# A cross-attention and feed-forward block: bias rows added by VectorE, or by accumulating SBUF transfers that GpSimd issues

## The reference

```python
x = x + (softmax(clip(q k^T * scale)) v) @ Wo + bo        # q from layernorm(x), k and v from the context; 16 heads
h   = layernorm(x) @ W1 + b1                              # 512 -> 2048
q   = h + (cos(theta)*w_re + sin(theta)*w_im) * (w_im * sin(theta + 0.1*h)) * 0.1
out = x + relu(q) @ W2 + b2                               # 2048 -> 512
```

## Time and profile before

| | |
|---|---|
| three runs | 1977.26, 1973.52, 1974.97 us; median 1974.97 us |
| span of the profiled execution | 1974.9 us (the page gives no other time for it; the span runs from the first to the last instruction) |
| TensorE | busy 1953.4 us, 99% of the span; mean granted clock 0.998 |
| VectorE | busy 1542.5 us, 78% |
| ScalarE | busy 1262.7 us, 64% |
| GpSimd | busy 517.0 us, 26%, nearly all of it in the first third |
| DMA | 441.29 MB, mean 223 GB/s; SP's queue takes 71.3% of the 16 engines' span |
| `add_row_bias` on DVE (L1827) | 28 instructions, 33.5 us |
| `add_last_bias` on DVE (L1835) | 32 instructions, 38.9 us |

### The profile page before, as it was taken

The page is one execution under the profiler, slowest core; times in us unless marked ns, Lnnn a source line. Parts: engine busy times, 40 slices in busy tenths (PEclk is TensorE's granted clock), DMA queues, the critical chain, the costliest instruction groups (busy, mean ns, idle before and its releaser), DMA issues.

```text
span 1974.9 us, 27897 instructions
## 1 busy us (share of the span) xinstructions
PE 1953.4 (99%) x9162; PEld 1620.3 (82%) x9162; DVE 1542.5 (78%) x2360; ACT 1262.7 (64%) x2132; POOL 517.0 (26%) x365
## 2 busy tenths in 40 slices
PE   9999999999999999999999999999999999999999
PEld 7788888888887788777888888788788888878887
DVE  8988888888876986888588768868858876886773
ACT  6767767767754876667367557647746755764762
POOL 6877777777774321000000000000000000000000
PEclk9999999999999999999999999999999999999999
DMA  7455565565545999778778878877977887786745
GB/s 239 147 164 158 160 165 146 163 173 150 156 111 161 333 351 298 255 224 256 277 236 246 263 257 249 256 268 236 260 282 233 244 261 258 241 262 221 236 150 192
DMA packets 347459, 441.29 MB, mean 223 GB/s; under 512 B 165552, under 2 KB 201392, under 8 KB 347312
## 3 DMA queue, kind: packets, MB, share of 16 engines
q1 hardware_dynamic: 346448, 439.44, 71.3%
q10 hardware_dynamic: 864, 0.04, 0.0%
HBM read 347.90 MB, written 91.23 MB: 222 GB/s over the span
## 4 chain that ended last, share of the span: by engine, by line
PE 76%; DVE 11%; ACT 6%; issue 4%; POOL 2%; DMA 1%; SPq 0%; DVEq 0%; ACTq 0%; POOLq 0%
PE psum L1985 25%; PE psum L1987 24%; PE psum L1986 24%; PE psum L2078 3%; DVE frac L1789 1%; ACT turns L1363 1%; DVE stats L1472 1%; ACT x_sb L1163 1%; ACT frac L1339 1%; DVE act_lo L1810 1%; DVE temps L1515 1%; DVE hid L1803 1%; DVE x_sb L1827 1%; ACT act_hi L1391 1%; DVE late_hid L1784 1%
## 5 line engine op out<-in xcount | busy, mean ns | idle before, releaser
L1985 PE MATMUL psum<-w_ring,act_hi 128*128 128x512 f32 x1024 | 400.3, 391 | 2.0 <-DVE act_lo L1810 1.4
L1987 PE MATMUL psum<-w_ring,act_lo 128*128 128x512 f32 x1024 | 398.6, 389 | 0.0
L1986 PE MATMUL psum<-w_ring,act_hi 128*128 128x512 f32 x1024 | 398.4, 389 | 0.0
L1985 PE MATMUL psum<-xo,w_ring 128*128 128x512 f32 x784 | 308.4, 393 | 5.5 <-ACT p_sb L1346 4.5
L1986 PE MATMUL psum<-xo,w_ring 128*128 128x512 f32 x784 | 305.9, 390 | 0.0
L1987 PE MATMUL psum<-xo,w_ring 128*128 128x512 f32 x784 | 305.9, 390 | 0.0
L886 POOL TENSOR_TENSOR rstd<-var_eps,minus_half 128x4 f32<-128x4 f32 x32 | 38.6, 1207 | 948.9 <-DVE var_eps L1479 944.1
L1985 PEld LDWEIGHTS psum<-w_ring,act_hi 128*128 128x128 f32 x1024 | 192.2, 188 | 49.2 <-issue 10.1
L1789 DVE SCALAR_TENSOR_TENSOR frac<-frac,turns 128x512 f32<-128x512 f32 x256 | 173.7, 690 | 74.5 <-ACT frac L1339 74.5
L1376 ACT ACTIVATE frac<-frac 128x512 f32<-128x512 f32 x256 | 156.6, 627 | 109.6 <-DVE frac L1789 109.6
L1987 PEld LDWEIGHTS psum<-w_ring,act_lo 128*128 128x128 f32 x1024 | 192.2, 188 | 40.3
(11 more groups left out here) (188 smaller groups left out, 4291.4 us busy)
## 6 DMA issues: line engine op xcount, KB each, us to landing
w_ring<-w2s SPq DMA_DIRECT2D x240, 512.0 KB, 3.7
w_ring<-w1s SPq DMA_DIRECT2D x392, 256.0 KB, 3.6
x_sb<-turn_dram SPq DMA_DIRECT2D x58, 512.0 KB, 6.2
res<-in_x SPq DMA_DIRECT2D x64, 256.0 KB, 3.7
x_dram<-res SPq DMA_DIRECT2D x64, 256.0 KB, 3.0
acc<-x_dram SPq DMA_DIRECT2D x16, 1024.0 KB, 7.1
x_sb<-in_x SPq DMA_DIRECT2D x15, 1024.0 KB, 6.1
x_sb<-x_dram SPq DMA_DIRECT2D x15, 1024.0 KB, 7.4
```

What stands on the lines that cost most here:

```text
L1985: pe.matmul(o, a_hi, b_hi, start=first, stop=False, skip_group_check=resumed)
L1986: pe.matmul(o, a_hi, b_lo, start=False, stop=False, skip_group_check=resumed)
L1987: return pe.matmul(o, a_lo, b_hi, start=False, stop=last, skip_group_check=resumed)
```

## The change

For the pairs' tiles, 26 transfers issued by POOL take the place of 52 DVE additions. Each is an SBUF-to-SBUF transfer with `accum_op=ALU.add`: its source is `bo_row` or `b2_row`, repeated for the four blocks, and its destination a whole tile of 1 MB (`x_sb[0]`, `x_sb[1]`, `acc[0]` or `acc[1]`) that already holds the loaded rows. Twelve go to `x_sb` (tiles 4 to 15) and fourteen to `acc` (tiles 2 to 15). DVE's consumers wait for the new semaphores `rows_added` and `out_added`. Tiles 0 to 3 of the row bias and tiles 0 and 1 of the output bias stay on DVE and POOL as before. Four pairs of semaphores are merged into one each, with the counts adjusted, which changes no instruction's place.

```diff
-            for T in range(4, TILES):
-                rsqrt(TILES + T)
+            def add_row_bias_by_dma(T):
+                pool.wait_ge(x_in[T % 2], x_loads(TILES + T))
+                pool.dma_start(x_sb[T % 2][:], bo_row[:].unsqueeze(1).to_broadcast([P, NB, C]), accum_op=ALU.add)\
+                    .then_inc(rows_added[T % 2], 16)
+
+            def add_last_bias_by_dma(T):
+                pool.wait_ge(acc_in[T % 2], 16 * (T // 2 + 1))
+                pool.dma_start(acc[:, T % 2], b2_row[:].unsqueeze(1).to_broadcast([P, NB, C]), accum_op=ALU.add)\
+                    .then_inc(out_added[T % 2], 16)
+
+            for T in range(1, FFN_PAIRS):
+                more = T + 1 < FFN_PAIRS
+                if more:
+                    add_row_bias_by_dma(2 * T + 2)
+                add_last_bias_by_dma(2 * T)
+                if more:
+                    add_row_bias_by_dma(2 * T + 3)
+                    rsqrt(TILES + 2 * T + 2)
+                    rsqrt(TILES + 2 * T + 3)
+                add_last_bias_by_dma(2 * T + 1)
...
+                    elif T > TILES + PLAIN + 1:
+                        dve.wait_ge(rows_added[T % 2], 16 * ((T - TILES) // 2 - 1))
                     elif T > TILES:
                         dve.wait_ge(x1_whole, whole_rows(T - TILES, n // 2))
...
-                    dve.wait_ge(acc_biased, 2 * T + n // 2 + 1)
+                    if T >= PLAIN:
+                        dve.wait_ge(out_added[T % 2], 16 * (T // 2))
+                    else:
+                        dve.wait_ge(acc_biased, 2 * T + n // 2 + 1)
...
-                    if p == (0 if T > 1 else 2):
-                        for half in range(2):
-                            add_last_bias(2 * T, half)
...
-                    if more and p == 0:
-                        for half in range(2):
-                            add_row_bias(2 * T + 2, half)
-                    if more and p in (2, 3):
-                        add_row_bias(2 * T + 3, p - 2)
-                    if p in (5, 7):
-                        add_last_bias(2 * T + 1, p // 6)
```

More of the change, by code:

```diff
@@ L298, in xattn_ffn @@
         vbd_in = sems("vbd_in", PAIRS)
-        bq_scaled = sem("bq_scaled")
+        bq_scaled = par_sin = sem("bq_scaled")
         mean_step, mean_moved = sem("mean_step"), sem("mean_moved")
-        par_step, par_sin = sem("par_step"), sem("par_sin")
+        par_step = sem("par_step")
         x_in = sems("x_in", XBUFS)
@@ L312, in xattn_ffn @@
         q_full_done, halves_done = sem("q_full_done"), sem("halves_done")
-        xn0_done = sem("xn0_done")
         x1_whole = sem("x1_whole")
@@ L322, in xattn_ffn @@
         y_psum, y_done = sem("y_psum"), sem("y_done")
-        nan_step, nan_psum, nan_count = (sem(n) for n in ("nan_step", "nan_psum", "nan_count"))
-        guard_done, last_done = sem("guard_done"), sem("last_done")
+        nan_step, nan_psum = sem("nan_step"), sem("nan_psum")
+        xn0_done = nan_count = nan_step
+        guard_done = last_done = sem("guard_done")
         fix_in, fix_add, fix_out = sem("fix_in"), sem("fix_add"), sem("fix_out")
@@ L336, in xattn_ffn @@
         acc_in, acc_biased, b2_biased = sems("acc_in", 2), sem("acc_biased"), sem("b2_biased")
+        rows_added, out_added = sems("rows_added", 2), sems("out_added", 2)
         SPLIT0 = 2 * KC
@@ L761, in load_rows @@
                 if T >= GUARDED:
-                    sp.wait_ge(last_done, 1)
+                    sp.wait_ge(last_done, 2)
                     for blk in range(NB):
@@ L978, in _ @@
                             .then_inc(w_lo_done, 1)
-            pool.wait_ge(nan_count, 1)
+            pool.wait_ge(nan_count, 4)
             count = pool.alloc_register("rows_without_nan")
@@ L1413, in _ @@
                         act.wait_ge(x1_stored[blk], 16 * TILES)
-                    act.wait_ge(last_done, 1)
+                    act.wait_ge(last_done, 2)
                 for n in later_chunks(j):
@@ L1685, in _ @@
                         dve.tensor_tensor(not_nan[:], squares[:], squares[:], ALU.is_equal).then_inc(nan_step, 1)
-                        dve.wait_ge(nan_step, 1)
+                        dve.wait_ge(nan_step, 2)
                         dve.tensor_reduce(row_ok[:], not_nan[:], AX_X, ALU.min).then_inc(nan_step, 1)
@@ L1848, in operand_sum @@
                 dve.tensor_tensor(PLACE[name], PLACE[a], PLACE[b], ALU.subtract).then_inc(t_done, 1)
-            dve.wait_ge(par_sin, 1)
+            dve.wait_ge(par_sin, 2)
             dve.wait_ge(par_step, PAR_REDUCED + 4)
@@ L1902, in _ @@
                         dve.wait_ge(x1_stored[blk], 16 * TILES)
-                    dve.wait_ge(last_done, 1)
+                    dve.wait_ge(last_done, 2)
                 for n in later_chunks(j):
@@ L2151, in _ @@
                 if i == GROUPS:
-                    pe.wait_ge(nan_step, 2)
+                    pe.wait_ge(nan_step, 3)
                     pe.matmul(psum[0:1, 0, 0:1], row_ok[:], ones[:], start=True, stop=True).then_inc(nan_psum, 1)
@@ L2215, in second @@
                 m.then_inc(f_psum, 1)
-            pe.wait_ge(nan_count, 1)
+            pe.wait_ge(nan_count, 4)
             pe.wait_ge(xn_done, TILES + 1)
```

## The result

The changed kernel took 1961.62 us (median of 4 runs, 1960.05 to 1962.60), the kernel before 1974.56 us beside it (4 runs, 1973.52 to 1977.26): a ratio of 0.9931 with a 95% interval of 0.9919 to 0.9943. That is faster by some 13 us (11 to 16 by the interval), where 9.8 had been predicted.

What follows compares the result with a forecast made beforehand. TensorE was taken to set the end, losing 14.2 us to VectorE's full list; 7.6 us back in pairs 2 to 6 and 2.2 in pair 1, with transfers at 0, took 1974.9 to 1965.1 us, range 1960 to 1997.

Steps and rivals of the forecast that it cites:

- full return: Rival: all 14.2 us that TensorE loses from 867 us on come back, giving 1960.7 us; chance 0.1.
- C: Start of step 6 of a pair: TensorE loses some 0.3 us, of which half, 0.15, was to return.
- D: Start of a pair's sweep: TensorE loses some 0.7 us waiting for late `act_lo`, of which 0.5 was to return.
- Pair 1: The first pair, from 867 us on: TensorE loses 3.2 us, of which 2.2 was to return.
- VectorE's busy time: Whole kernel: 52 bias additions of about 1.2 us go, so VectorE's busy time falls by some 62 us.
- A: Start of step 2 of a pair: TensorE loses 0.38 us with the matmul behind it; all was to return.
- B: Start of step 5 of a pair: TensorE loses 0.49 us waiting for ScalarE's `p_sb`; all was to return.
- GpSimd: Issues 26 transfers, otherwise idle in the pairs; even 3 us each ends by step 1, delaying nothing wanted earlier.
- The new waits: Consumers of accumulated tiles: 1 MB taken to land in 15 us, between 7 and 40; only 40 would delay statistics.
- The DMA cost of 0: Near a pair's start: SP's queue keeps up at half of 394 GB/s, 7.6 us to spare for weight slots, costing 0.
- The starved ring: Rival: late weight slots stall TensorE 3.9 us in step 1 or 2, plus 1.3 slow clock; 1996 us, chance 0.30.
- Relief that isn't used: Rival: ScalarE is late by itself, so little returns; 1971.6 us or later; chance 0.14, shared with a small starvation.

Runs made afterwards that it cites:

- odd_rows: Kernel before, with only the row bias of each pair's odd tile added by transfer (VectorE's additions of steps 2 and 3 gone): 1963.33 us, ratio 0.9944.
- even_outs: Kernel before, with only the output bias of each pair's even tile added by transfer (two of VectorE's step 0 additions gone): 1966.46 us, ratio 0.9957.
- odd_outs: Kernel before, with only the output bias of each pair's odd tile added by transfer (additions of steps 5 and 7 gone): 1967.97 us, ratio 0.9960.
- outs_x2: Changed kernel with each even tile's output-bias transfer issued twice, 1 MB more per pair: 1977.87 us, ratio 1.0012.
- moved: Kernel before, no bias transfers, with the even tile's two output additions in steps 4 and 6 instead of step 0: 1979.71 us, ratio 1.0024.
- outs_only: Changed kernel with only the fourteen output-bias transfers kept; VectorE adds the row bias again: 1960.10 us, ratio 0.9922.
- spaced: Changed kernel with the even tile's output-bias transfer issued behind the pair's first `rsqrt`, so only two accumulations meet the loads: 1962.05 us, ratio 0.9936.
- spaced_tile1: Changed kernel with the even output-bias transfer behind the pair's first `rsqrt`, and tile 1's output bias also added by transfer: 1962.00 us, ratio 0.9934.

## Why the prediction was right, and what was mis-sized

The mechanism is the predicted one: TensorE at the pace of one matmul per 0.2267 us is the floor, the losses are VectorE's lag, and they go. The sum was 9.8 us; the traces show 14.2 back, the new stall of 0.6 already taken off, and the medians 13. That is "full return", which had 0.1 of the chances. So the mechanism was right, and the term that was mis-sized is the share of each loss that comes back (C, D and pair 1 below).

- **VectorE's busy time**, predicted down by some 62 us: its records add up to 61.1 us less, but its busy time fell only from 1542.5 to 1493.0 us, 49.5, because records that follow each other at once overlap by some 0.08 us (two halves of 1.22 us take 2.35), and there are fewer such places now. The starts are back at 0.23 us in pairs 2 to 6.
- **A**, 0.38: right; what TensorE waits for is VectorE's `hidden_22` of step 1.
- **B**, 0.49: right, and odd_rows, which takes the additions of steps 2 and 3, shows it. But relief in step 0 alone removes it too (even_outs): the lag is carried, which the prediction did not use.
- **C**, 0.15 of 0.3: mis-sized, and the wait was misread. All of it went. "ScalarE's normalization stands there too" was no obstacle: TensorE waits for VectorE's `hidden_12`, and the addition of step 5 stands right ahead of that (1.22 us at 1566.02). odd_outs, without this addition, loses nothing there.
- **D**, 0.5 of 0.7: mis-sized. All of it went. "The first can profit only from what step 5 gives back" was the step that failed: odd_rows takes nothing from steps 5 and 7 and still removes every late loss, by the lag of steps 2 and 3.
- **Pair 1**, 2.2 of 3.2 us: behind 867 us all of it came back; ahead of it stands the new stall of 0.6 us.
- **The relief as shares.** The errors in D and pair 1 are one: I gave each wait a share of what stands right ahead of it. But lag is carried from step to step, and a wait is gone as soon as the lag is below the room ahead of TensorE (1.7 us at step 5); further relief is worth nothing.
- **GpSimd**: an issue takes 1.28 us, 1.85 for the second of a burst; nothing waits behind it. "At most 3 us each" held.
- **The new waits**: the accumulation was taken as 15 us; alone it takes 10.5 to 15.2, behind another in flight mostly 18.5 to 27. VectorE has no wait for a transfer in the pairs.
- **The DMA cost of 0** came out as 0.6 us, but the cover was thinner than I wrote. The prediction had SyncE's queue at half of 394 GB/s; it got 142 of 268. Near the pair's start, where 8 us had been predicted, the slots for the 9th to 21st product of pair 5 land in 7.4 to 14.7 us, 11.5 in the median (6.1 over the whole kernel), and of the 7.6 us to spare 0.3 are left in pairs 2 to 6 and none once in pair 1.
- **The starved ring**, 0.30: its mechanism is what the counts show (queues in turn, 142 GB/s where it had 131), and its length was wrong: the packets of the 3 MB run for 25 us (1467.2 to 1492.2), not 36, so SyncE falls back by 1.2 MB, not 2.2. "Decides from 7.6 us of added landing time" fits: with 0.3 us left nothing is lost in pairs 2 to 6, and with 1 MB more (outs_x2) they lose 1.7 us each. "A stall of such length brings the clock down" held in most traces, not in all: the wait of 2.5 us at the start of pair 1 was followed by a clock of 0.50 before and after, but not in outs_x2 and moved (last section).
- **Relief that isn't used**: its reason "in steps 0 to 3 the waits for ScalarE swallow what VectorE saves" is refuted by even_outs, where the loss at 29 us and that of step 5 go. (B in half is 5 x 0.25 = 1.2 us, not 1.5; it changes nothing.)

No version measured beats the changed kernel beyond the spread. outs_only (1960.10 us) has the lowest median, but its interval (0.9905 to 0.9939) covers that of the changed kernel; it needs 14 transfers instead of 26 and leaves 2.1 us or more before each slot of `w1_ring` is read, so of the equal ones I would keep it, or spaced.

## What to carry to other kernels

An engine that feeds a saturated one has a tolerance at each wait: work out its lag step by step against the other's pace. Relief pays until the lag is inside the tolerance, and nothing from there on; it can come from any earlier step from which the lag is carried, and work put into a step without room costs more than it did elsewhere. So try the smallest part of a change first; here 14 transfers do what 26 do. And before work is put on the DMA engines, compare each landing of the most urgent stream with the time until it is read, not the mean share: 1 MB more per pair turned a gain of 13 us into a loss of 2 to 3.

## What the runs showed of the hardware

- An accumulating transfer from SBUF to SBUF goes in 2 KB packets of 179 ns; 1 MB lands in 10.5 to 15.2 us when it is alone in its queue. The same transfer without the addition goes in 4 KB packets of 173 ns and lands in 6.0 to 8.3 us alone: the addition doubles the engines' time (7.6% of the span against 3.7%).
- Two busy queues got the same number of packets (1265 to 1264 in 20 us), so that the one with the larger packets got more bytes, and a queue that needs 193 GB/s got 142.
- Waits of TensorE under 1 us left the granted clock at 1.00: so it stands in every window of a pair from 2 to 6 of outs_x3, which hold 26 of its 28 waits, and at 1500 to 1516 us of outs_x2, with two waits of 0.47 us. Behind waits of 2.1 to 2.5 us it differed from case to case: the wait for `p_sb` at the start of pair 1 (2.5 us, in spaced_tile1 2.1) was followed by a stretch at 0.50 in the traces of twelve of the fourteen kernels, and by none in outs_x2 and moved; in outs_x2 a wait of 2.35 us at 850 us was followed by 0.50, in spaced_tile1 one of 2.3 us at 829 us was not. The stretch costs 1.6 us (before, eight distances between starts that are 0.2 us longer), as much as some differences in the table of runs.

The windows around the 2.5 us wait of pair 1 in outs_x2 and in moved:

```profile
800.00:812.00 12.00, 9.49 (x42) 7.54 (x42) 9.09 (x10) 6.16 (x9) 0.00 (x0) 1.00 0.67 204
```

```profile
805.00:815.00 10.00, 7.48 (x33) 5.91 (x33) 6.48 (x9) 5.54 (x9) 0.00 (x0) 1.00 0.82 262
```

and from outs_x2, two of TensorE's short waits and the window around them:

```profile
1509.83 0.50 PE L2002 MATMUL psum<-xo,w_ring 128*128 128x512 f32 x1 [0.47 <-DMA w_ring<-w1s]
1511.96 0.50 PE L2002 MATMUL psum<-xo,w_ring 128*128 128x512 f32 x1 [0.47 <-DMA w_ring<-w1s]
```

```profile
1500.00:1516.00 16.00, 15.06 (x66) 11.80 (x65) 12.12 (x20) 10.82 (x18) 0.87 (x1) 1.00 1.09 283
```
